# A hand-ordered Mamba block: eight tiles in each turn of the loop in place of two, and six tiles written out ahead of it

## What is computed

```python
def step(h, inp):                    # one chunk of 128 rows, 8 chunks a sequence
    x_c, d_c, B_c, C_c = inp
    A_bar = jnp.exp(d_c[..., None] * A)
    BX = d_c[..., None] * B_c[:, :, None, :] * x_c[..., None]
    log_A_cum = jnp.cumsum(jnp.log(jnp.maximum(A_bar, EPS)), axis=1)
    ...
    h_chunk = A_cum * wcum / jnp.maximum(A_bar, EPS) + h[:, None] * A_cum
    y_c = jnp.einsum('bls,blds->bld', C_c, h_chunk) + D_param * x_c
    return (h_chunk[:, -1], y_c)
...
x = x + mamba(layernorm(x))          # in_proj, conv, silu, proj, softplus, step, gate, out_proj
x = x + int8_matmul(layernorm(x), rhs)
```

## Time and profile before

| what | value |
| --- | --- |
| time, median of 3 runs | 5796.58 us |
| the profiled execution | 5795.46 us, its span 5793.5 us |
| PE busy | 5611.7 us, 97% of the span |
| DVE busy | 5350.9 us, 92% |
| ACT busy | 3733.7 us, 64% |
| POOL busy | 2456.2 us, 42% |
| granted TensorE clock, mean | 0.992 |

### The profile page before, as it was taken

One profiled execution on the slowest core, in us unless ns is written; L12 is line 12 of the kernel. 1 busy time (PEld: TensorE's weight loads), 2 busy tenths in 40 slices (PEclk: granted clock), 3 DMA queues, 4 the chain that ended last, 5 costly groups with the idle time before them and its releaser, 6 DMA issues. The chain is left out here.

```text
span 5793.5 us, 78230 instructions
## 1 busy us (share of the span) xinstructions
PE 5611.7 (97%) x16088; PEld 2641.4 (46%) x16152; DVE 5350.9 (92%) x7057; ACT 3733.7 (64%) x4615; POOL 2456.2 (42%) x2139
## 2 busy tenths in 40 slices
PE   8999999999999999999999999999999999999997
PEld 3444444444444444444444444444444444444443
DVE  7999999999999999999999999999999999999997
ACT  5666666666666666666666666666666666666664
POOL 3444444444444444444444444444444444444443
PEclk9999999999999999999999999999999999999999
DMA  2212212112121121121211212212112121121220
GB/s 69 19 16 16 20 14 18 16 15 20 14 18 18 16 18 16 15 20 14 18 17 15 20 14 17 20 14 18 16 15 20 14 18 17 17 18 16 15 18 12
DMA packets 158421, 104.23 MB, mean 18 GB/s; under 512 B 121024, under 2 KB 121024, under 8 KB 158016
## 3 DMA queue, kind: packets, MB, share of 16 engines
q1 hardware_dynamic: 158016, 100.71, 19.0%
HBM read 42.63 MB, written 16.78 MB: 10 GB/s over the span
## 5 line engine op out<-in xcount | busy, mean ns | idle before, releaser
L496 POOL TENSOR_SCALAR room<-total,limit 128x1024 f32<-128x1024 f32 x1024 | 1182.9, 1155 | 3244.6 <-PE cum L1068 475.1
L754 ACT ACTIVATE decay<-cum,neg_a 128x1024 f32<-128x1024 f32 x1024 | 1137.4, 1111 | 1539.2 <-PE cum L1068 1535.4
L1078 PE MATMUL state<-sources,tri_upto 128*128 128x512 f32 x4096 | 1971.8, 604 | 124.4 <-DVE term L1415 124.0
L1068 PE MATMUL cum<-step,tri_before 128*128 128x512 f32 x4096 | 1937.4, 595 | 0.1
L1415 DVE SCALAR_TENSOR_TENSOR term<-state,crow,decay 128x1024 f32<-128x1024 f32 x1024 | 1312.8, 1282 | 313.4 <-PE state L1078 197.1
L1425 DVE TENSOR_TENSOR acc<-acc,term 128x1024 f32<-128x1024 f32 x1024 | 1362.3, 1330 | 0.2
L1402 DVE SCALAR_TENSOR_TENSOR sources<-cum,brow,dx 128x1024 f32<-128x1024 f32 x1024 | 1305.8, 1275 | 7.2 <-ACT cum L770 7.2
L1068 PEld LDWEIGHTS cum<-step,tri_before 128*128 128x128 f32 x4096 | 780.1, 192 | 963.9 <-issue 939.2
L770 ACT ACTIVATE cum<-room,pos_a 128x1024 f32<-128x1024 f32 x1024 | 1143.5, 1117 | 108.9 <-POOL room L496 100.1
L1078 PEld LDWEIGHTS state<-sources,tri_upto 128*128 128x128 f32 x4096 | 742.5, 190 | 995.5 <-issue 867.8
L485 POOL TENSOR_SCALAR step<-delta,limit 128x1024 f32<-128x1024 f32 x1024 | 1144.5, 1118 | 42.7 <-DVE delta L1317 42.7
(11 more groups left out here) (127 smaller groups left out, 3626.3 us busy)
## 6 DMA issues: line engine op xcount, KB each, us to landing
hfirst<-hrows SPq DMA_DIRECT2D x496, 64.0 KB, 3.9
xt<-in_x SPq DMA_DIRECT2D x64, 256.0 KB, 2.6
hrows<-term SPq DMA_DIRECT2D x1024, 4.0 KB, 1.7
xres<-in_x SPq DMA_DIRECT2D x64, 256.0 KB, 2.6
out_x<-xres SPq DMA_DIRECT2D x64, 256.0 KB, 2.1
gate_last<-gate SPq DMA_DIRECT2D x512, 0.5 KB, 2.1
hrows<-hrows SPq DMA_DIRECT2D x64, 64.0 KB, 2.3
win<-in_w_in SPq DMA_DIRECT2D x2, 1024.0 KB, 7.9
```

The costliest lines, as they stand in the source:

```text
L496: nc.gpsimd.tensor_scalar(room[:, :], total[:, :], limit[:, s:s + 1], 0.0, ALU.min, ALU.max).then_inc(limited, 1)
L754: nc.scalar.activation(decay[s % 4][:, :], cum[s % 2][:, :], ACT.Exp, scale=neg_a[:, s:s + 1]).then_inc(decay_ready, 1)
L1068: last = nc.tensor.matmul(cum[s % 2][:, cols], tri_before[:, :], step[s % 2][:, cols], start=True, stop=True)
L1078: last = nc.tensor.matmul(state[:, cols], tri_upto[:, :], source[s % 2][:, cols], start=True, stop=True)
```

## The change

The frame of all five engines is rewritten: two more tiles (4 and 5) are written out ahead of the loop, and a turn holds the bodies of four pairs. The loop now takes p = 3, 7, ..., 27: seven turns for tiles 6 to 61, six branches back. Nothing else differs; every line below L314 moves down by three.

```diff
             body(Tile(1, 0), True, True)
             body(Tile(1, 1), True, True)
-            with eng.Fori(2, PAIRS - 1) as p:
-                body(Tile(p, 0), True, True)
-                body(Tile(p, 1), True, True)
+            body(Tile(2, 0), True, True)
+            body(Tile(2, 1), True, True)
+            with eng.Fori(3, PAIRS - 4, 4) as p:
+                for q in range(4):
+                    body(Tile(p + q, 0), True, True)
+                    body(Tile(p + q, 1), True, True)
             body(Tile(PAIRS - 1, 0), True, False)
             body(Tile(PAIRS - 1, 1), False, False)
```

## The result

The changed kernel takes 5757.87 us, the median of three runs (5749.38 to 5758.18), against 5796.58 us before: a ratio of 0.993, with a 95% interval of 0.9908 to 0.9953. It is faster by 0.7%, 38.7 us. The forecast was 5745 us with a range of 5708 to 5780. So the sign and the range came out, and the gain is 38.7 us where 51.6 was forecast; the terms behind them did not all do so, and the experiments sort them.

What follows compares the result with a forecast made beforehand. PE was taken to bound the kernel, idle mainly waiting for DVE, which stops at the branch back. Terms: 71.5 + 14.1 - 30 - 4 = 51.6 us gained; 5795.5 - 51.6 + 1.1 = 5745 us, range 5708 to 5780.

Steps and rivals of the forecast that it cites:

- What bounds the kernel: PE's matmuls set the pace; PE waits 124.0 us for DVE's `term_of`, reachable where DVE stops at the branch back.
- Branches back and the clock behind them: At turn ends, 22 fewer branches back gain 71.5 us, and 22 x 0.64 of half clock gains 14.1 us.
- PE's code no longer stays: PE fetches its longer loop every turn; 15 late branches at its `If`s, 2.0 us each, lose 30 us.
- The fit of where a piece begins: In PE's code, pieces begin at remainder 199 modulo 256; branches at 3,081, 6,382 and 8,924 are late.
- PE's own branch back: Six times it misses, some 3.3 us, mostly hidden by the wait for DVE: nothing taken, 12 us if uncovered.
- DVE late at its `If`s: One DVE branch of the eight in a turn may come late: between nothing and 20 us, 4 taken as lost.
- Others fetch theirs anew in every turn: In the kernel before, PE keeps its loop's code while other engines refetch; jumps cost ACT 2.5 us, DVE 2.9.
- No branch of PE is late in the loop: Rival: PE's jumps in the loop cost nothing, giving 5711 us, or 5707 with 3.46 a branch; chance 0.20.
- More late branches: Rival: four of PE's eight `If`s a turn are late, 58 us lost in place of 30, 5773 us; chance 0.17.
- all late: Rival: every `If` of PE is late, 57 branches losing 114 us against 85.6 gained, 5825 us; chance 0.06.
- the wait only moves: Rival: DVE stops wherever it takes up new code, so no change, about 5795 us; chance 0.05.
- The signs that I named for a wrong prediction: Long `If`s at other tiles or far more; PE standing longer than DVE at its branch back; DVE stopping inside turns.

Runs made afterwards that it cites:

- e1_dve_eight: The kernel before with DVE alone at eight tiles a turn (six written out in front), the other engines at two: 5723.69 us, ratio 0.9873.
- e1_act_eight: The kernel before with ACT alone at eight tiles a turn (six written out in front), the other engines at two: 5797.65 us, ratio 1.0001.
- e1_pe_two: The changed kernel with PE left in the form of before, two tiles a turn, the other four engines at eight: 5726.17 us, ratio 0.9878 to before.
- e2_pe_shift: The changed kernel with 24 semaphore increments on PE ahead of its loop, so the loop's code stands 24 instructions later: 5738.24 us, ratio 0.9902 to before.
- e2_all_flat: The kernel before with all 64 tiles written out on all five engines, no branch back on any: 5699.18 us, ratio 0.9834.
- e2_pe_four: The kernel before with DVE at eight tiles a turn and PE at four, ACT, POOL and SP at two: 5749.51 us, ratio 0.9920.

## Why the prediction came out as it did

**What bounds the kernel:** right. The gain is DVE's stop at the branch back, and nothing of ACT's (e1_dve_eight, e1_act_eight).

**Branches back and the clock behind them, 85.6 us gained:** mis-sized; e1_pe_two measures 5797.1 - 5726.2 = 70.9. The step that failed is the price of a plain tile. I took 87.46 from the earlier trace rows, the tile from 591.08 to 678.54. It stands right behind a stop, and DVE's clock starts late in it. PE's `states` of slot 0 at its two ends, in the kernel before:

```profile
587.47 1.98 PE L1078 MATMUL state<-sources,tri_upto 128*128 128x512 f32 x4 [2.46 <-DVE term L1415]
...
675.48 1.94 PE L1078 MATMUL state<-sources,tri_upto 128*128 128x512 f32 x4
```

L1414 stands 3.61 us behind the first and 3.06 behind the second, so by PE the tile takes 88.01 us. A tile with no stop on either side takes 87.72 in the changed kernel, by PE as by DVE. So an end saved isn't worth the whole difference of 90.92 and 87.46, and 42 tiles at 0.33 account for 14 of the 14.7 us missing.

**PE's code no longer stays, 15 late `If`s at 2.0 us, 30 us lost:** the mechanism is right, the count and the price are not. Seven in the loop are late, one a turn, at 20 us by e2_pe_shift, 2.9 each. Against the same two tiles in e1_pe_two the four with the clock at 1.00 behind them cost 2.3 us each, near the 2.0 forecast; the other three cost 3.8, since the half clock, which the price left out, adds 1.5. The fit of where a piece begins named three positions; 8,924 was late in every turn, 6,382 (424 ns) and 3,081 (429 ns) never. So fifteen at 2.0 made 30 us where seven at 2.9 make 20. The fit was made on one late branch, and said so; e2_pe_shift shows that the place in the piece matters, e2_all_flat that it doesn't decide alone.

**PE's own branch back, "I take nothing":** this is the step that failed outright. It was hidden behind a wait for DVE of 2.42 us. But PE reaches its branch 3.5 us before DVE reaches its own (1286.0 against 1289.5), stands there itself, then again at the `If`, whose code isn't there either, and then works at half clock; DVE's wait is what became hidden. It costs 12 us against e1_pe_two, by chance the 6 x 2.0 that I named for the case that the cover was gone. Where only DVE goes back with PE, six such ends cost nothing in sum (e2_pe_four): some 1 us each, set off by a clock that didn't fall.

**DVE late at its `If`s, 4 us:** not seen. At a branch back DVE's stop stands not in the branch, which lasts 62 ns (1289.5), but between it and the next instruction, 2.8 to 3.1 us. Behind the `If`'s branch the next instruction of DVE starts within 0.21 us in every tile of the loop.

**"Others fetch theirs anew in every turn":** in the kernel before this holds for DVE and ACT only. POOL's and SP's sequencers went on within 0.32 us of their branches back there; in the changed kernel they stop for 2.4 to 3.0 us. The four engines with long loops and PE in its short one (e1_pe_two, 5726.2) come out close to DVE alone with its long loop (e1_dve_eight, 5723.7).

In sum: 70.9 - 20 - 12 = 38.9 us, and 38.7 was measured; forecast were 85.6 - 30 - 0 - 4 = 51.6. The forecast was 13 us too low because the gain was 15 too large and PE's branch back 12 too cheap, while the `If`s were 10 too dear and DVE's 4 us weren't there. That the time fell well inside the range is in part luck: errors of 27 us on the one side and 14 on the other partly cancel.

**The rivals.** "No branch of PE is late in the loop" falls, and with it the reading that a jump of 259 instructions hardly ever stalls: it lasted 3.3 to 3.7 us seven times in a loop whose code didn't stay. "More late branches" falls with seven in place of its 28, "all late" and "the wait only moves" with the plain tiles of 87.72. The signs that I named for a wrong prediction are there in one point: PE stands at its own branch back longer, 3.5 to 4.0 us, than DVE does at its own. (In the first rival the time with 3.46 a branch is 5796.6 - 90.2 = 5706, not 5707.)

## What to carry to other kernels

The length of a turn is a choice for each engine. An engine whose loop doesn't stay in any case, and which the busiest one waits for at the branch back (here DVE, not ACT), gains by fewer branches back, or none; one whose loop stays (here PE, with 1,700 instructions) has nothing to gain, and once its loop is too long it pays at the branch back and at some of the jumps; so look at which queue moves instructions while the loop runs before unrolling all engines alike. And take the price of an undisturbed step from a step that has undisturbed steps on both sides: the one behind a stall looked too cheap here, by 0.25 us. And read it on the engine that sets the pace: a clock on another engine can show a loss one tile late.

## What was unexpected

PE's limit lies between 1,700 instructions (branch back 0.2 us, nothing on q8 while the loop runs) and 3,395 (3.6 us, 233 packets). Twenty-four instructions that do nothing, in front of a loop, made the kernel 19.6 us faster by moving one `If` of the loop in its piece of code. The granted clock's stay at 0.50 behind a joint branch back was some 3.4 us in two turns and over 6 in the other four, and the ends of the latter are 2 us longer; what decides between them wasn't found. Nor was it found why the clock fell behind three of the seven late `If`s and not behind the other four.

The Trainium skill (Runtime: NRT & Kernel Launch, section Instruction fetch mechanics) gives branch stalls as a reason to unroll fully. On DVE this case agrees (5794.8 to 5696.0 us with DVE alone written out); with PE written out too the kernel takes 5699.2, and with PE left in its short loop 5680.9, so on PE the measurement says otherwise.
